# Moving the residual add of two dense stages from VectorE to GpSimd

## The reference, cut to what matters

```python
h = (x + agg / deg) @ W.T + b
hn = (h - mean(h)) * rsqrt(var(h) + 1e-05) * g + beta
x = x + silu(hn)
...
updated = node_states @ W_self.T + b_self + aggregate @ W_msg.T + b_msg
normed = (updated - mean) * rsqrt(var + 1e-05) * ln_gamma + ln_beta
x = x + gelu(normed)
```

## Time and profile before

| what | value |
|---|---|
| three runs, median (lowest to highest) | 5131.09 us (5129.94 to 5133.36) |
| the profiled execution's own time | 5129.8 us |
| its span, first to last instruction | 5128.1 us |
| PE busy | 4200.7 us (82%) |
| DVE busy | 3366.2 us (66%) |
| POOL busy | 2535.6 us (49%) |
| ACT busy | 1359.9 us (27%) |
| second dense stage, first work to the end of its loop | 2555.4 to 2664.2 us |
| third dense stage, the same | 4709.6 to 4806.9 us |

### The profile page before, as it was taken

How to read it: one execution, slowest core, us unless ns; L and a number is a source line. 1 busy time by engine, 2 the same in 40 slices (tenths; PEclk the granted TensorE clock), 3 DMA queues, 4 the chain that set the end, 5 groups by cost and what they waited for, 6 DMA issues and landing times. The chain is left out here.

```text
span 5128.1 us, 77007 instructions
## 1 busy us (share of the span) xinstructions
PE 4200.7 (82%) x20133; PEld 3514.9 (69%) x20134; DVE 3366.2 (66%) x8997; ACT 1359.9 (27%) x4238; POOL 2535.6 (49%) x2647
## 2 busy tenths in 40 slices
PE   6787877777777999999866999999288888888359
PEld 3486655665656888988755888888166666666258
DVE  8987877877777777777675111111778777786841
ACT  5385000000044444444263222222200000002512
POOL 0002777777725777777601222222257777774221
PEclk8898999999999999999998999999589999999779
DMA  3201333333323333333412222211723333332620
GB/s 94 46 1 33 105 105 104 105 104 104 105 62 109 106 106 106 106 106 106 132 44 98 70 78 93 93 52 44 228 81 104 104 104 104 104 104 81 203 60 19
DMA packets 250615, 476.19 MB, mean 93 GB/s; under 512 B 61052, under 2 KB 155053, under 8 KB 250422
## 3 DMA queue, kind: packets, MB, share of 16 engines
q0 software_dynamic: 126848, 345.69, 23.3%
q1 hardware_dynamic: 118374, 123.01, 7.7%
q10 hardware_dynamic: 5200, 5.24, 0.3%
HBM read 490.23 MB, written 69.36 MB: 109 GB/s over the span
## 5 line engine op out<-in xcount | busy, mean ns | idle before, releaser
L1064 PE MATMUL sum_sums<-sum_got,sum_onehot 128*128 x9408 | 2193.3, 388 | 426.6 <-SPq L114 293.8
L1064 PEld LDWEIGHTS sum_sums<-sum_got,sum_onehot 128*128 128x128 f32 x9408 | 1774.8, 192 | 807.4 <-issue 574.1
L997 POOL DMA_INDIRECT sum_got<-xn,edge_row x1568 | 1496.1, 954 | 1068.9 <-DVE edge_row L1094 544.7
L1276 DVE TENSOR_TENSOR acc<-acc,sum_sums 128x256 f32 (+1 forms) x2352 | 990.8, 421 | 602.9 <-PE sum_sums L1064 342.4
L997 POOL DMA_INDIRECT sum_got<-h,edge_row x784 | 741.1, 945 | 349.1 <-issue 238.5
L789 ACT ACTIVATE xb<-xb,edge_weight 128x98 f32<-128x98 f32 x1568 | 430.9, 363 | 509.0 <-DVE xb L759 507.8
L2082 DVE TENSOR_TENSOR moe_f_y<-moe_f_ps_y,moe_b 128x256 f32<-128x256 f32 x112 | 42.3, 420 | 670.5 <-PE moe_f_ps_y L2026 670.5
L1222 DVE TENSOR_SCALAR sum_onehot<-iota,sum_now 128x128 f32<-128x128 f32 x1584 | 425.8, 362 | 7.5
L1232 DVE TENSOR_SCALAR sum_onehot<-iota,sum_now,ones 128x128 f32<-128x128 f32 x1584 | 424.3, 368 | 7.1
L2011 PE MATMUL moe_f_ps_h<-moe_f_xT,xb 128*128 128x256 f32 x1792 | 424.7, 380 | 0.0
L2026 PE MATMUL moe_f_ps_y<-xb,moe_f_hT 128*128 128x256 f32 x1792 | 422.7, 379 | 0.0
(11 more groups left out here) (508 smaller groups left out, 3925.0 us busy)
## 6 DMA issues: line engine op xcount, KB each, us to landing
xb<-in_L_ffn_W SPq DMA_DIRECT2D x112, 1024.0 KB
sum_got<-xn,edge_row POOLq DMA_INDIRECT x1568, 2.7
xn<-xb SPq DMA_DIRECT2D x21, 896.0 KB, 4.1
sum_got<-h,edge_row POOLq DMA_INDIRECT x784, 2.7
moe_out_c_got<-moe_rows SPq DMA_DIRECT2D x49, 256.0 KB, 3.1
h<-xb SPq DMA_DIRECT2D x7, 896.0 KB, 4.2
x<-acc SPq DMA_DIRECT2D x7, 896.0 KB
pair<-xb SPq DMA_DIRECT2D x7, 896.0 KB
```

The costliest lines, as they stand in the source:

```text
L997: pool.indirect_dma_start(got[:, c % SU, 0:D], None, source, bass.IndirectOffsetOnAxis(ap=p.edge_row[:, c:c + 1], axis=0)).then_inc(s_got[ ...
L1064: mm = nc.tensor.matmul(sums[k % 2][j], onehot[:, ((k % 2) * HALF + j) * PAIR + r, :], pair[:, r, :], start=(r == 0), stop=(r == PAIR - 1))
L1276: v.tensor_tensor(a, a, sums[k % 2][j], ALU.add).then_inc(s_added[j], 1)
```

## The change

The add of the old rows moves from VectorE's stream to a new stream of GpSimd, which runs over the 49 tiles and waits for the activation and for the old rows of each. VectorE takes the statistics of tile n - 13 in step n, now behind a wait for GpSimd's sum, and its loop has one step more, which takes the last tile's statistics. The waits of ScalarE and SP for the sum stay as they are.

```diff
-SCALE_LAG, ACTIVE_LAG, SUM_LAG = 9, 10, 12
+SCALE_LAG, ACTIVE_LAG, STATS_LAG = 9, 10, 13
...
-            for n in range(NT + (SCALE_LAG if residual is None else SUM_LAG)):
+            for n in range(NT + (SCALE_LAG if residual is None else STATS_LAG)):
...
-                if residual is not None and at_step(n, SUM_LAG):
-                    t = n - SUM_LAG
-                    dve.wait_ge(s_active, t + 1)
-                    dve.wait_ge(s_old[t % U], 16 * (t // U) + 16)
-                    v.tensor_tensor(p.acc[:, t, 0:D], active[:, t % U, :], old[:, t % U, :], ALU.add).then_inc(s_summed, 1)
-                    if t >= 1:
-                        dve.wait_ge(s_summed, t)
-                        c.done(norm2.take(p.acc[:, t - 1, 0:D], t - 1))
+                if residual is not None and at_step(n, STATS_LAG):
+                    t = n - STATS_LAG
+                    dve.wait_ge(s_summed, t + 1)
+                    c.done(norm2.take(p.acc[:, t, 0:D], t))
             if residual is not None:
-                dve.wait_ge(s_summed, NT)
-                c.done(norm2.take(p.acc[:, NT - 1, 0:D], NT - 1))
                 c.settle()
...
         else:
+            @block.gpsimd
+            def _(pool):
+                for t in range(NT):
+                    pool.wait_ge(s_active, t + 1)
+                    pool.wait_ge(s_old[t % U], 16 * (t // U) + 16)
+                    nc.gpsimd.tensor_tensor(p.acc[:, t, 0:D], active[:, t % U, :], old[:, t % U, :],
+                                            ALU.add).then_inc(s_summed, 1)
+
             @block.sync
```

## The result

On one chip, 20 executions of each kernel: 5139.27 us after the change against 5131.24 us before, a ratio of 1.0017 (95% interval 1.001 to 1.0023). That is 8.0 us more by the medians, and between 5 and 12 by the interval. The forecast was 4.4 us less. The move cost time where it was to win a little.

What follows compares the result with a forecast made beforehand. VectorE was taken to bound the second stage and both tails, TensorE the third stage's middle. Terms of 0, 0 and -4.4 us took 5129.8 to 5125.4, or 5126.7 as median; range 5116 to 5140.

Steps and rivals of the forecast that it cites:

- Which instructions collide: Both dense stages: GpSimd's add stops VectorE's put and scale, up to 0.9 us; product and statistics pass at 0.42.
- the rival in which GpSimd stops every VectorE instruction: Both stages: the add holds up product and statistics too; +9.2 us, 5140.3, chance 0.10.
- the one in which nothing collides: Both stages: short adds fall between VectorE's statistics and product; -14.7 us, 5116.4, chance 0.13.
- The add's price: Both stages: one add of 256 columns on GpSimd takes 0.60 us, between 0.53 and 0.66.
- The formula for the step: Second stage's ordinary step: 1.18 us plus the add's time, 1.78 us as before, so a term of 0.
- The rival of a long add: Both stages: an add of 0.90 us gives +11.5 us, 5142.6; decides from about 0.71 us; chance 0.10.
- the prediction's own sum: Whole kernel: second stage 0, third stage's middle 0, tails -4.4 us.
- About 21 of 49 adds are really paid for: Second stage: 21 adds cost VectorE 0.34 us each; the rest lie in waits for ScalarE or the tail.
- The third stage at zero: Third stage's middle: VectorE's step of 1.38 us stays below TensorE's 1.51, so a term of 0.
- The tails: After the last matmul of each stage: the reduction starts 2.2 us earlier, -4.4 us for both.
- What was costed at nothing: Both stages: old-row loads, GpSimd's queue, waits of ScalarE and VectorE for the sum, and the first add after gathers; no cost.
- the prediction's own signs of being wrong: Both stages: puts of 0.48 us beside GpSimd, growing products or statistics, adds over 0.7 us, groups changing by over 0.5 us.

Runs made afterwards that it cites:

- run 3: The changed kernel, but GpSimd's add of each tile also waits for the next tile's scale; 0.9975 of the kernel before.
- run 5: The changed kernel, but GpSimd adds only the first 128 columns of each tile, the other half left out; 0.9982 of the kernel before.
- the late add: The kernel of run 3, in which GpSimd's add also waits for the next tile's scale; measured twice, 0.9975 and 0.9976 of the kernel before.
- run 4: The changed kernel, but GpSimd fills 768 unused columns with a constant instead of adding, reading nothing from SBUF; 0.9972 of the kernel before.
- Run 6: The late add for tiles 0 to 36, with VectorE adding the last twelve tiles; 0.9983 of the kernel before.
- run 1: The kernel before, with the adds moved to GpSimd in the second dense stage alone; 1.0011 of the kernel before.

## Why the prediction was wrong

**Which instructions collide: right.** Put and scale grow to 0.95 us (1.01 behind a table change) and a put ends 0.29 us after the add (forecast: up to 0.9, 0.27). Product and statistics pass: in the second stage's middle they last at most 0.426 and 0.422 us. There an add lies beside about half of a product at most and beside no statistics. But the 17 products of run 3's second stage that lie wholly within an add last at most 0.427 us, and the statistics within an add in the tail 0.42. That rules out the rival in which GpSimd stops every VectorE instruction; puts of 0.95 us rule out the one in which nothing collides.

**The add's price: wrong.** The prediction took 0.60 us, between a proportional 0.53 and 0.66 with the iota's 0.134 as a fixed part, and called both the bounds. Over both stages it is:

```profile
L1584 POOL TENSOR_TENSOR acc<-gnn_g_active,gnn_g_old x98: 717/727/912, 2579.1 to 4813.3; 128x256 f32<-128x256 f32 x98
```

The median is 0.727 us, above the upper bound. With the 0.46 us for 128 columns of run 5 it gives some 2.1 ns a column and a fixed part of 0.19 us; with the 3.70 us for 1792 columns it gives 1.94 ns and 0.23. An iota of one element is no bound for the fixed part of an add. The formula for the step, 1.18 plus the add, held at both lengths: 1.91 for 1.93 measured, 1.64 for 1.66. So 0.15 us a step is lost where zero was forecast. The rival of a long add named this mechanism and where it decides, 0.71 us; the add lies just above it. But the price alone explains little. Put into the prediction's own sum, 0.73 us gives 21 x 0.13 = 2.7 us in the second stage, nothing in the third and -0.9 in each tail: some 1 us slower, where the profiled execution lost 7.9 outside the lead-ins. The size comes from the next two steps.

**"About 21 of 49 adds are really paid for": wrong.** The prediction held that in the steps behind a table change VectorE has idle time, and that a change there costs nothing. But two adds come there close together, and the second stops the put of the very step that ScalarE had delayed. Of the 1.10 us that a group loses, the two steps behind the table change make 0.38 (4.91 us from scale to scale for 4.53), the five others the rest. So the whole group pays, 1.10 us, and not four of its seven adds, 0.6: over the middle 5.9 us without the clock, for 21 x 0.15 = 3.2. In run 3, with the add out of the way, that put is back at 0.47 us.

**The third stage at zero: wrong.** The prediction compared VectorE's step of 1.38 us with TensorE's of 1.51, and so saw a reserve of 0.13 in VectorE. Both steps were read rightly. What failed is the step from there to the group: TensorE's seven steps are 10.6 us and the group is 11.70, and the difference, TensorE's wait for ScalarE's copy, was taken to stay whatever VectorE does. It hangs on VectorE, as rows of the kernel before show which the prediction did not read:

```profile
4766.79 0.42 DVE L558 BATCH_NORM_STATS2 n2stats<-acc 128x6 f32<-128x256 f32 x1
...
4768.10 0.60 PE L1475 MATMUL gnn_g_psout<-xb,ident 128*128 128x256 f32 x2
4768.18 0.42 DVE L558 BATCH_NORM_STATS2 n2stats<-acc 128x6 f32<-128x256 f32 x1
...
4769.35 0.42 ACT L1510 ACTIVATE gnn_g_active<-gnn_g_scaled 128x256 f32<-128x256 f32 x1 [0.34 <-DVE gnn_g_scaled L1561]
...
4769.62 0.60 PE L1475 MATMUL gnn_g_psout<-xb,ident 128*128 128x256 f32 x2
4769.79 1.28 ACT L1513 ACT_TABLE_LOAD   x1
```

VectorE takes 1.39 us from statistics to statistics without idle time, TensorE 1.52 from one tile to the next. Each of ScalarE's activations waits for VectorE's scale (0.34 us idle), and its table load starts 0.02 us behind the last of them. So VectorE's steps set when the table change starts, and behind the change TensorE waits. Where VectorE's step changes, the group follows: 1.54 us and a group of 12.60 after the change, 1.39 and 11.70 before, 1.27 and 11.26 with half the add, 1.18 and 10.80 with the late add. (By the prediction's own formula the step after the change is 0.78 plus 0.73, 1.51.) There it ends: in run 4, with a step of 1.05, it is 10.80 too, six steps of TensorE of 1.52 us and one of 1.70. That is TensorE's own pace, 0.90 us below the kernel before. The loss of a group, 0.90 us, comes to 4.45 in the middle.

**The tails: right in sign, too large.** -2.2 us each were forecast, -1.4 and -1.5 measured. Ten adds take 8.05 us, not the 6.0 and 1.6 of the sum, and the first starts 3.61 us behind the last product (2656.51 to 2660.12), not 3.26 (2650.61 to 2653.87); together 0.8 us. From the last scale to the reduction it was 3.81 us, not 2.1. Run 6 prices the same term at 1.1.

**What was costed at nothing.** Old rows, ScalarE's wait and the queues did not show: GpSimd's idle time in the second stage's middle all ends with the activation. One part of the loss belongs to none of these terms: TensorE's clock fell in one group of the profiled execution after the change (2591.36 to 2606.57, 15.21 us for 14.79 in the next), 0.4 us of the 6.35.

**The sum.** The forecast was 0, 0 and -4.4. Measured, without the lead-ins, were +6.35 in the second stage's middle, +4.45 in the third's and -2.9 in the tails: +7.9. The forecast had the wrong sign, since each of the three terms was taken too favourably: the middles at nothing, the tails at half as much again as they gave. That 5139.27 lies in the range, 5116 to 5140, is luck: its upper end came from the rival in which GpSimd stops every VectorE instruction, which the runs rule out. Two of the prediction's own signs of being wrong came: adds of over 0.7 us, and groups that change by over 0.5 us.

## What to carry to other kernels

An add given to GpSimd, which reads SBUF, stopped VectorE's instructions with two SBUF inputs until it had ended, so place it in time: held back by one wait until VectorE is at instructions with one SBUF input, the very same add turned a loss of 0.17% into a gain of 0.25%. In a loop with periodic interruptions compare whole periods, not single steps, and follow who waits for whom into the interruption: an engine with the shorter step can still set the period. And the price of a short instruction is not bounded by scaling a long one and adding the smallest instruction at hand.

## What the runs showed of the hardware that was not expected

GpSimd's float32 add of 128 columns takes 0.46 us, of 256 columns 0.73 us, of 1792 columns 3.70 us: some 0.2 us fixed. The stop goes both ways: back to back beside VectorE's scales the add took 0.90 us, and ten of them 8.05 us, six beside a scale.

A GpSimd instruction that only writes SBUF (0.74 us) leaves VectorE's two-input instructions at 0.48 us.

TensorE's granted clock can fall to 0.50 (1.2 GHz) for some 3 us after a table change of ScalarE, in one execution of a kernel and not in another. Its four matmuls of a tile then take 1.91 us instead of 1.03, and a group of seven tiles 0.71 us more in the late add, 0.4 in the kernel after the change. It fell in slower kernels than the one before (once after the change, twice in run 1) and in faster ones (four times in one profiled run of the late add and not once in the other).
